# Two token tiles of a transformer group in one PSUM bank, with the three instruction lists ordered anew

## The reference

```
h = patches @ Wp.T + bp
h = layernorm(h + attention(h))      # 12 heads of 64, window of 65 keys, zero padding, softmax, w_out, b_out
h = layernorm(h + experts(h))        # 3 causal attention experts of width 64, the best 2 weighted per token, Wp, bp
```

## Time and profile before

| | |
|---|---|
| times of three runs | 121.11, 121.96 and 561.58 us; median 121.96 |
| the profiled execution | 121.46 us, span of its trace 119.7 us |
| granted TensorE clock, mean | 0.997 of full speed |
| busy: PE, DVE, ACT, POOL | 109.4, 76.8, 71.4, 21.5 us |
| HBM read, written | 7.14 MB, 0.44 MB |

### The profile page before, as it was taken

The page is one execution under the profiler, slowest core; times in us unless marked ns, Lnnn a source line. Parts: engine busy times, 40 slices in busy tenths (PEclk is TensorE's granted clock), DMA queues, the critical chain, the costliest instruction groups (busy, mean ns, idle before and its releaser), DMA issues.

```text
span 119.7 us, 3567 instructions
## 1 busy us (share of the span) xinstructions
PE 109.4 (91%) x1411; PEld 97.0 (81%) x1411; DVE 76.8 (64%) x232; ACT 71.4 (60%) x196; POOL 21.5 (18%) x32
## 2 busy tenths in 40 slices
PE   6979999999999999999999899999868999897940
PEld 4769998987799888889998899899767898795930
DVE  0467848730582844593876776876847678998581
ACT  4469855459938758654458666652364485447450
POOL 6003614471400910000007900000000000000000
PEclk9999999999999999999999999999999999999998
DMA  3999999100000000000000000000000000000102
GB/s 92 255 362 404 416 424 398 43 0 5 3 0 5 3 0 0 5 0 5 0 5 0 0 0 5 0 5 0 0 3 0 8 0 5 0 5 0 54 20 74
DMA packets 3675, 7.80 MB, mean 65 GB/s; under 512 B 844, under 2 KB 1996, under 8 KB 3532
## 3 DMA queue, kind: packets, MB, share of 16 engines
q1 hardware_dynamic: 3660, 7.59, 17.6%
HBM read 7.14 MB, written 0.44 MB: 63 GB/s over the span
## 4 chain that ended last, share of the span: by engine, by line
PE 66%; DVE 16%; ACT 5%; issue 5%; DMA 4%; SPq 2%; DVEq 0%; ACTq 0%
PE proj L846 10%; PE score L913 8%; PE outp L944 6%; PE outp L813 4%; PE proj L831 4%; DMA x_f<-x_t 4%; PE trans L923 4%; PE proj L835 3%; PE proj L832 3%; PE score L813 3%; PE proj L838 3%; PE proj L839 3%; PE score L902 2%; PE proj L969 2%; DVE ln_st L670 2%
## 5 line engine op out<-in xcount | busy, mean ns | idle before, releaser
L478 ACT ACTIVATE pt_t<-trans,image_t 108x216 f32<-108x216 f32 (+1 forms) x48 | 16.5, 419 | 2.3 <-PE trans L923 2.3
L469 ACT ACTIVATE score<-d_t 128x296 f32<-128x296 f32 (+1 forms) x16 | 6.7, 418 | 10.8 <-DVE d_t L635 10.7
L913 PEld LDWEIGHTS score<-k_t,q_t 64*36 64x36 f32 x480 | 10.3, 111 | 3.1 <-issue 1.4
L913 PE MATMUL score<-k_t,q_t 64*36 64x37 f32 (+1 forms) x480 | 12.1, 196 | 0.1
L644 DVE TENSOR_REDUCE sm_t<-score 128x8 f32<-128x288 f32 x16 | 7.2, 449 | 7.6 <-ACT score L469 7.5
L632 DVE TENSOR_REDUCE mx_t<-score 128x8 f32<-128x296 f32 (+1 forms) x16 | 7.3, 456 | 4.5 <-PE score L913 4.4
L969 PE MATMUL proj<-wo_hi,x_hi 128*108 128x192 f32 (+1 forms) x36 | 9.5, 264 | 0.0
L971 PE MATMUL proj<-wo_lo,x_hi 128*108 128x192 f32 (+1 forms) x36 | 9.2, 256 | 0.0
L974 PE MATMUL proj<-wo_hi,x_lo 128*108 128x192 f32 (+1 forms) x36 | 9.2, 256 | 0.0
L444 ACT ACTIVATE q_t<-proj 128x288 f32<-128x288 f32 x12 | 4.9, 410 | 6.5 <-PE proj L839 6.3
L499 ACT ACTIVATE ln_ln<-ln_mv,const 108x1 f32<-108x1 f32 (+1 forms) x12 | 3.5, 294 | 8.6 <-DVE ln_mv L673 8.6
...
## 6 DMA issues: line engine op xcount, KB each, us to landing
...
```

Of the source, the lines that this page charges most:

```text
L478: nc.scalar.activation(pt_t[:, n % 2, 0:tiles, :, i], trans[0:ROWS, 0:tiles, :, 0:TOK], ACT.Copy, scale=image_t[:, i:i + 1]).then_inc(spli ...
L913: ins = nc.tensor.matmul(s[64 * h:64 * h + TOK, im, 0:width], q, k_t[rows, n % QK_RING, im, 0:width], start=False, stop=True, skip_group_c ...
```

## The change

Token tiles 0 and 1 of a group, 192 columns each, share one bank (`SHARED`): tile 0 in columns 0 to 191, tile 1 in 192 to 383. One bias product with 384 columns, issued with tile 0, opens both. Tile 1 takes no bank of its own. Since two tiles now lie in the bank that DVE reads, the statistics of tile 0 wait until both sums are complete, and the bank is free when both tiles' `ap` are done. This holds for both layers and both groups. The three lists are ordered anew; their rows tell little by themselves, so one line of each stands here, and three places are shown behind the diff.

```diff
+SHARED = [(0, 1), (0, 1), (2,)]
...
-em 0, em 1, em 2, em 3, em 4, em 5, em 6, qk 0, em 7, em 8, em 9, qk 1, s 0, v 0 0, s 1, em 10, em 11
+em 0, em 1, em 2, em 3, em 4, em 5, em 6, qk 0, em 7, s 0, em 8, qk 1, em 9, qk 2, s 1, v 0 0, em 10, s 2
...
-sp 7, cq 10, ex 9, sp 8, cg 0, sp 9, ex 10, oh 7, cq 11, oh 8, ex 11, sp 10, oh 9, oh 10, sp 11, ge 0
+h1 0, oh 7, cq 10, ex 9, sp 8, cg 0, sp 9, ex 10, cq 11, oh 8, ex 11, oh 9, sp 10, oh 10, sp 11, ge 0
...
-ap 1 0, ap 1 1, st 1 2, ap 1 2, cn 12, h1 1, sh 12, nm 12, sh 13, nm 13, gd 1, cn 14, ol 12, ol 13, sh 14
+ap 1 0, ap 1 1, st 1 2, ap 1 2, cn 12, h1 1, sh 12, nm 12, sh 13, nm 13, cn 14, gd 1, ol 12, ol 13, sh 14
...
-            elif kind == "outa":
-                plan("out", key, (tok_s, norms.index(("", *key)) + 1))
-            elif kind == "res2":
-                plan("out2", key, (tok_s, norms.index(("2", *key)) + 1))
+            elif kind in ("outa", "res2"):
+                layer, (g, t) = "" if kind == "outa" else "2", key
+                if t == 1:
+                    uses[("out" + layer, key)] = uses[("out" + layer, (g, 0))]
+                else:
+                    plan("out" + layer, key, (tok_s, max(norms.index((layer, g, u)) for u in SHARED[t]) + 1))
...
+        def token_sums(layer, g, t):
+
+            return bank("out" + layer, (g, t))[0:tile_rows(t), DIM * (t == 1):DIM * (t == 1) + DIM]
...
-                dve.wait_ge(summed, sums.index((layer, g, t)) + 1)
-                link(nc.vector.bn_stats(ln_st[0:rows, t], bank("out" + layer, (g, t))[0:rows, 0:DIM]))
+                dve.wait_ge(summed, max(sums.index((layer, g, u)) for u in SHARED[t]) + 1)
+                link(nc.vector.bn_stats(ln_st[0:rows, t], token_sums(layer, g, t)))
...
-                nc.tensor.matmul(b[0:rows, 0:DIM], ones_r[:, 0:rows], rows_r[:, layer], start=True, stop=False,
-                                 skip_group_check=True)
+                if t != 1:
+                    count = len(SHARED[t])
+                    both = bank(("out", "out2")[layer], (g, t))[0:rows, 0:count * DIM]
+                    nc.tensor.matmul(both.rearrange("p (j d) -> p j d", d=DIM), ones_r[:, 0:rows],
+                                     rows_r[:, layer].unsqueeze(1).broadcast_to([128, count, DIM]), start=True,
+                                     stop=False, skip_group_check=True)
```

More of the change, by code:

```diff
@@ L89 @@
+t 0, em 11, v 0 1, qk 3, v 0 2, t 1, rows 0, s 3, qk 4, pv 0, v 1 0, pv 1, qk 5, s 4, t 2, v 1 1, t 3, s 5
+pv 2, t 4, v 1 2, qk 6, pv 3, qk 7, s 6, pv 4, t 5, s 7, qk 8, pv 5, outa 0 0, outa 0 1, outb 0 0
+outb 0 1, t 6, s 8, outa 0 2, pv 6, outb 0 2, t 7, qk 9, tr 0, s 9, pv 7, qk 10, t 8, s 10, gate 0, t 9
+qk 11, pv 8, s 11, fv 0 0, pv 9, t 10, fv 0 1, lg 0, pv 10, t 11, outa 1 0, pv 11, outa 1 1, outb 1 0
 outb 1 1, outa 1 2, outb 1 2, qk 12, tr 1, s 12, qk 13, gate 1, s 13, t 12, qk 14, lg 1, pv 12, t 13
-fv 1 0, qk 15, pv 13, s 14, s 15, fv 1 1, res2 0 0, one2 0 0, out2 0 0, res2 0 1, one2 0 1, out2 0 1, t 14
@@ L91 @@
[L91 to L92 removed]
+qk 15, pv 13, fv 1 0, s 14, fv 1 1, res2 0 0, one2 0 0, s 15, res2 0 1, one2 0 1, out2 0 0, out2 0 1
+res2 0 2, one2 0 2, out2 0 2, t 14, t 15, pv 14, tr2 0, res2 1 0, pv 15, one2 1 0, res2 1 1, one2 1 1
+out2 1 0, out2 1 1, res2 1 2, one2 1 2, out2 1 2, tr2 1
 """
 ACT_ORDER = """
[L95 removed]
@@ L682, in normalise_tokens @@
                     dve.wait_ge(projected, ready[("tr" + before, (g0, 1))])
-                src = bank("out" + layer, (g, t))[0:rows, 0:DIM]
+                src = token_sums(layer, g, t)
                 mean, rstd = ln_mv[0:rows, t, 0:1], ln_rs[0:rows, t]
@@ L968, in add_pair @@
                 pe.wait_ge(o_hi_s, n + 1)
-                nc.tensor.matmul(b[0:rows, 0:DIM], o_hi[:, g, p, cols], wo_hi[:, p, 0:DIM], start=False, stop=False,
+                nc.tensor.matmul(b, o_hi[:, g, p, cols], wo_hi[:, p, 0:DIM], start=False, stop=False,
                                  skip_group_check=True)
-                nc.tensor.matmul(b[0:rows, 0:DIM], o_hi[:, g, p, cols], wo_lo[:, p, 0:DIM], start=False, stop=False,
+                nc.tensor.matmul(b, o_hi[:, g, p, cols], wo_lo[:, p, 0:DIM], start=False, stop=False,
@@ L972, in add_pair @@
                                  skip_group_check=True)
                 pe.wait_ge(o_lo_s, n + 1)
-                return nc.tensor.matmul(b[0:rows, 0:DIM], o_lo[:, g, p, cols], wo_hi[:, p, 0:DIM], start=False,
+                return nc.tensor.matmul(b, o_lo[:, g, p, cols], wo_hi[:, p, 0:DIM], start=False,
                                         stop=(p == PAIRS - 1), skip_group_check=True)
@@ L978, in project_out @@
                 pe.wait_ge(wo_lo_s, 1)
[L979 to L980 removed]
+                if t != 1:
+                    take("out", (g, t))
+                residual(g, t, 0)
                 for p in range(PAIRS - 1):
[L982 removed]
+                    add_pair(g, t, p)
             def project_out_last(g, t):
[L985 removed]
+                add_pair(g, t, PAIRS - 1).then_inc(summed, 1)
             def expert_residual(g, t):
[L988 removed]
+                if t != 1:
+                    take("out2", (g, t))
+                residual(g, t, 1)
             def project_experts(g, t, c):
[L992 to L993 removed]
+                b, n = token_sums("2", g, t), ENTRY_OF[("ffn", g, c)]
+                cols, w = tile_cols(t), slice(F_PROJ, F_PROJ + DIM)
                 pe.wait_ge(o_hi_s, n + 1)
[L995 removed]
+                nc.tensor.matmul(b, y_hi[:, g, c, cols], ffn_hi[:, c, w], start=False, stop=False,
                                  skip_group_check=True)
                 if c == 0:
[L998 removed]
+                    nc.tensor.matmul(b, y_hi[:, g, c, cols], ffn_lo[:, w], start=False, stop=False,
                                      skip_group_check=True)
                 pe.wait_ge(o_lo_s, n + 1)
[L1001 removed]
+                ins = nc.tensor.matmul(b, y_lo[:, g, c, cols], ffn_hi[:, c, w], start=False,
                                        stop=(c == 1), skip_group_check=True)
```

43 lines of the change are left out of this document (16 added, 27 removed).

## The result

The changed kernel took 124.97, 124.99 and 124.91 us (one further execution, 130.13 us at a mean granted clock of 0.939, was disturbed and is left out, as such executions are in all times below), the kernel before 121.53 us in the median of four, one of which took 561.58 us. Ratio 1.0281, 95% interval 1.0244 to 1.0319: slower, beyond the 2% bound and above the range that ended at 124.1 us. The profiled execution took 124.97 us, its span is 123.1 us, 3.4 us more than before.

What follows compares the result with a forecast made beforehand. TensorE's queue was taken to bound the kernel, busy 109.4 of 119.7 us. Terms 0.0 + 0.33 + 0.28 + 0.24 + 0.19 = +1.04 us on 121.46 gave 122.5 us, range 120.4 to 124.1.

Steps and rivals of the forecast that it cites:

- Stage A: Start to `pv 5`: 0.5 us wait for POOL before `qk 2`, offset by savings of 0.33 and 0.18; sum 0.0.
- The two credits of stage A: Before `outa 0 0`: 0.33 us from the old gap before `qk 2`, 0.18 from one fewer interruption of wide products.
- Stage B: Group 0's layer norm, to `outa 1 0`: later statistics delay `tr 0` by 0.5 us, plus an interruption; sum +0.33 us.
- part comes back: Behind `tr 0`: `s 9` and `pv 7` cover the 0.3 us for which `qk 10` waited, leaving net +0.15.
- TensorE never stops: Between `tr 0` and `outa 1 0`: no waits, only one more interruption, +0.18 us.
- Stages C: Group 1's layer norm: statistics wait for three more products, nothing covers it, and all behind moves; +0.28 us.
- D: Experts of group 1: DVE waits 0.44 us for convolution taps, 0.20 us of another wait goes; +0.24 us.
- the tail: Last layer norm to store: `st2 1 0` waits for the two products of `out2 1 1`, nothing hides it; +0.19 us.
- The signs: New profile: listed waits and DVE's first L677 at about 59.0; wrong if TensorE's busy time is off by over 0.5 us.
- the first, better lists: Whole kernel: the new lists are better and it gets a little faster, sum -0.8, 120.6 us; chance 0.36.
- The second: Sharing costs more than lists hide: `st 0 0`'s 1.98 us delay all passes to `tr 0`, 124.3 us; chance 0.14.

Runs made afterwards that it cites:

- E12: Changed kernel with DVE's two subtractions of the value weights reading their first operand from PSUM instead of SBUF; one time, 123.68 us.
- E4: Changed kernel with DVE's low part of the value weights (`wv 0`) moved behind `xs 11`; ratio 1.0237 to the kernel before.
- E5: Changed kernel with ScalarE's `wq 2` moved ahead of `wv 0`, so POOL gets weight pair 2 sooner; ratio 1.0197 to the kernel before.
- E7: Changed kernel with the old order between `tr 0` and `t 11` on TensorE, ScalarE and DVE; ratio 1.0268 to the kernel before.
- E2: Kernel before, a bank for each tile, with the three new lists; ratio 1.0207 to the kernel before.
- E1: Changed kernel, shared bank, with the three old lists; one time, 125.10 us.
- E8: Shared bank, old lists except the new order between `outa 0 0` and `tr 0` on TensorE and ScalarE, and `st 0 0` behind `nm 7` on DVE; ratio 1.0179.

## Why the prediction was wrong

**Stage A, the failing step.** "Its two instructions took from 19.44 to 20.25 + 0.82, 1.63 us, so it ends at 19.1": I took POOL's duration from a place where DVE did other work, and moved it to one where DVE reads two operands from SBUF. It took 2.62 us, and the wait is 1.48 us counted from 18.66, beyond my bound of 1.0. E12 shows the cause, E4 and E5 the effect. Without the collision 0.49 us of stage A's 1.74 are left, close to the 0.5 that the forecast gave the wait. The trace of before had the same collision one pair earlier and smaller, 0.95 and 0.83 us where POOL alone took 0.73, in rows that I did not read, timelines of POOL and DVE of the kernel before:

```profile
13.68 0.95 POOL L367 TENSOR_TENSOR wqk_lo<-wqk_f,wqk_hi 128x256 fp32r<-128x256 f32 x1
14.71 0.83 POOL L369 TENSOR_TENSOR wqk_hi<-wqk_f,wqk_hi 64x256 fp32r<-64x256 f32 x1
...
13.20 1.75 DVE L584 TENSOR_TENSOR x_lo<-x_f,x_hi 128x288 fp32r<-128x288 f32 x3
```

The two credits of stage A, 0.33 for the gap before `qk 2` and 0.18 for an interruption, came to nothing or nearly: E5, with no wait left, stands at 0.0, not at -0.5.

**Stage B, the second one.** The chain to `tr 0` was priced nearly right (0.5, measured 0.65, since DVE's idle time did take up most of the 2.17). Wrong was "part comes back" and "TensorE never stops". `s 9` and `pv 7` do cover `qk 10`'s wait, 0.28 us by `s 10`; then `s 10`, now right behind `qk 10` and `t 8`, waits for its k copy, and `t 9` for `nm 9`, whose exponential stands behind that copy on ScalarE: 0.8 us together. E7 shows that the old order loses 0.32 us of this before `qk 10` and 0.46 in all.

**Stages C, D and the tail** were right in mechanism and place: E2, with separate banks, has 0.01 in C and 0.02 in the tail, against 0.27 and 0.14. D's size was off: 0.07 us at `tr2 0` instead of 0.24.

**The signs.** Of those listed for the new profile, the waits came: 1.18 us before `qk 2` (forecast 0.5), 0.69 before `tr 0` (0.7 to 1.2), 0.50 for the taps (0.4), 0.9 of L838 for L694 (over 0.6). DVE's first L677 stood at 60.78, not 59.0. TensorE's busy time is 0.9 us higher, which was named as a sign of being wrong. And the low end of the bounds was added up wrong: A's -0.5, B's -0.15 and D's -0.4 below 122.5 give 121.4 to 121.5, not 121.2; the range does not hang on it.

**The rivals.** Of the first, better lists, nothing was seen: E2 has them alone and is slower. The second gave 124.3 us, near the result, for a reason that did not hold, so its nearness is luck: `st 0 1` ended 0.49 us later than stage A alone explains, not 1.6. E1 shows where it would have held, in the old order, and there through `qk 9`'s bank. The Trainium skill (Perfetto Trace Analysis, Matmuls), which asks for rotation through banks, agrees with E1 in direction: with the sharing and the old lists 3.3 us were lost by `outa 1 0`, 2.23 of them in one wait for the shared bank. It agrees less with E8, where 1.06 were left once TensorE had other steps to do.

Open remains why the lag at `outa 0 0`, loads taken off, is 1.5 to 1.75 us in kernels with the same early rows, and what takes the 0.5 to 0.7 us behind `tr 0` with the new rows and 0.3 to 0.5 with the old ones.
